# Layer 0 routing and experts in one block, the shared expert under the routing chain

## The reference, cut to what matters

```python
x = layernorm(x + L0_attn(x))
# L0_ffn: 64 experts of width 88, 8 groups of 8 experts, 4 groups and 8 experts kept
scores = sigmoid(x @ gate_w.T);  choice = scores + gate_bias
group_scores = sum of the two largest of choice in each group of 8
masked = choice where the group is among the best 4, else 0
topk_idx = the 8 largest of masked;  topk_w = scores[topk_idx]
rw = topk_w / (sum(topk_w) + 1e-20) * 2.5            # 0 for the other experts
routed = sum_e rw[:, e] * (silu(x @ Wg[e].T) * (x @ Wu[e].T)) @ Wd[e].T
shared = (silu(x @ Sg.T) * (x @ Su.T)) @ Sd.T        # width 176, every token
x = layernorm(x + routed + shared)
```

## Time and profile before

| | |
|---|---|
| median of 3 runs | 1407.01 us (1405.93 to 1410.32) |
| the profiled execution, its own time | 1402.02 us |
| its span | 1400.3 us |
| PE busy over the span | 1279.3 us (91%) |
| DVE | 1114.2 us (80%) |
| ACT | 898.5 us (64%) |
| POOL | 481.3 us (34%) |
| moved by DMA | 135.87 MB |

### The profile page before, as it was taken

How to read it: one execution, slowest core, us unless ns; L and a number is a source line. 1 busy time by engine, 2 the same in 40 slices (tenths; PEclk the granted TensorE clock), 3 DMA queues, 4 the chain that set the end, 5 groups by cost and what they waited for, 6 DMA issues and landing times. The chain is left out here.

```text
span 1400.3 us, 21389 instructions
## 1 busy us (share of the span) xinstructions
PE 1279.3 (91%) x7374; PEld 711.9 (51%) x7374; DVE 1114.2 (80%) x1726; ACT 898.5 (64%) x1503; POOL 481.3 (34%) x988
## 2 busy tenths in 40 slices
PE   5898987169999999999889999999999998999998
PEld 2222224157777777777643232223222337777776
DVE  5677763758999999999758788888889747688886
ACT  4988873034555555555453788888888866767775
POOL 4565551014334343334142244224422422221210
PEclk8898988579999999999999999999999999999999
DMA  5422200064666666666236555434342201121200
GB/s 156 127 56 66 63 21 7 0 134 110 147 143 154 148 151 151 147 146 152 79 113 146 111 156 133 121 102 104 88 123 61 53 11 52 62 91 46 91 31 31
DMA packets 70020, 135.87 MB, mean 97 GB/s; under 512 B 13031, under 2 KB 44328, under 8 KB 63112
## 3 DMA queue, kind: packets, MB, share of 16 engines
q1 hardware_dynamic: 68760, 133.46, 37.5%
q10 hardware_dynamic: 1152, 1.05, 0.2%
HBM read 116.87 MB, written 16.29 MB: 95 GB/s over the span
## 5 line engine op out<-in xcount | busy, mean ns | idle before, releaser
L1589 ACT ACTIVATE a_PR<-n1a_C 128x512 f32<-128x512 f32 x576 | 299.6, 603 | 79.5 <-PE n1a_C L1495 79.4
L1604 DVE CUSTOM_DVE_ANT_0 OC_last<-a_mring,a_COR 128x1024 bf16<-128x1024 f32 x256 | 302.6, 1218 | 42.4 <-PE a_mring L1462 42.1
L1432 POOL TENSOR_SCALAR_AFFINE_SELECT a_PR<-a_PR 128x128 f32<-128x128 f32 x512 | 136.2, 296 | 250.2 <-ACT a_PR L1589 249.7
L868 ACT ACTIVATE e_HH<-e_H 128x512 fp32r<-128x512 f32 x184 | 116.4, 633 | 158.3 <-DVE e_H L916 157.5
L1495 PE MATMUL n1a_C<-a_QP,a_KP 74*128 74x512 bf16 (+3 forms) x768 | 176.1, 332 | 4.4 <-ACT a_PR L1589 3.5
L402 ACT ACTIVATE a_PR<-a_ring,a_ng 128x1024 f32<-128x1024 f32 (+1 forms) x160 | 150.2, 1045 | 26.0 <-PE a_ring L345 26.0
L427 DVE TENSOR_SCALAR a_PR<-a_PR,a_lo,a_hi 128x1024 f32<-128x1024 f32 (+1 forms) x160 | 119.2, 763 | 56.1 <-ACT a_PR L402 55.6
L1514 PE MATMUL n1a_C<-a_PR,a_V 128*9 128x512 f32 (+3 forms) x1536 | 152.1, 492 | 0.0
L887 DVE TENSOR_TENSOR e_HL<-e_H,e_HH 128x512 fp32r<-128x512 f32 x138 | 139.4, 1010 | 13.5 <-DVE e_H L904 0.5
L810 POOL TENSOR_TENSOR e_HL<-e_H,e_HH 128x512 fp32r<-128x512 f32 x46 | 78.5, 1706 | 180.5 <-ACT e_HH L868 180.5
L1883 DVE TENSOR_TENSOR e_HL<-e_GL,e_HH 128x512 fp32r<-128x512 f32 x144 | 109.5, 765 | 38.3 <-ACT e_HH L1851 34.7
(11 more groups left out here) (257 smaller groups left out, 2252.6 us busy)
## 6 DMA issues: line engine op xcount, KB each, us to landing
e_ROUTE<-routing SPq DMA_DIRECT2D x24, 704.0 KB
a_QP<-q_parts SPq DMA_DIRECT2D x72, 192.0 KB
e_RAW<-in_w_chunks SPq DMA_DIRECT2D x46, 192.0 KB, 7.4
a_QM<-q_parts SPq DMA_DIRECT2D x64, 128.0 KB, 2.8
e_GATE<-gates SPq DMA_DIRECT2D x8, 1024.0 KB, 4.4
e_ROUTE<-routing SPq DMA_DIRECT2D x8, 640.0 KB
a_KP<-k_parts SPq DMA_DIRECT2D x24, 192.0 KB
e_ROUTE<-routing SPq DMA_DIRECT2D x8, 576.0 KB
```

Of the source, the lines that this page charges most:

```text
L868: nc.scalar.activation(HH[n % NH][:], HT[n % NH][:], ACT.Copy).then_inc(high_done, 1)
L1432: last = nc.gpsimd.affine_select(out=d, in_=d, compare_op=keep, fill=0.0, base=0, pattern=[[step, P]], channel_multiplier=-step)
L1589: nc.scalar.activation(PR[:, g % NPR, j, :], ring[n % NRING][:], ACT.Exp).then_inc(s_read, 1)
L1604: nc.vector.tensor_tensor_reduce(out=junk[:, i % 2, :], in0=mring[k % 2][:], in1=COR[:, c:c + S], scale=1.0, scalar=-3.0e38, op0=ALU.mult, ...
```

## The change

`route_l0` and `experts_l0` become one block, `moe_l0`, and part of the work in front of it moves into `normalise("n0a")`.

- Inside `n0a`: PE makes the logits of each token group as it is normalised, ACT makes the high half of X and, at the end, the four sigmoids, POOL makes the low half of X and the splits of chunks 0 to 2. SP loads the gate weights and the first four chunks.
- The DVE chain of the routing is rewritten (the two largest of 8 by pairwise maxima and minima), and `link(..., then)` puts products of items into it: 20 in all.
- PE makes gate and up of items 0 to 19 while the chain runs, then turns the routing weights; ACT copies them out of PSUM.
- Items are weighed 20 behind their product (`BEHIND`), their low half follows one item later, `down` runs 23 behind. 24 buffers `T` hold what is between. The shared items are added with one matmul in plain float32 from RAW, without high and low halves.
- There are 4 RAW buffers and 8 slots of split weights, instead of 3 and 3; still 3 buffers `ROUTE`. The low halves on POOL come 6 chunks behind the split. In the last 20 items POOL makes every second low half instead of every fourth.
- In `project_l1` five `keep_busy` matmuls are added behind the third group's `down`, and the last 16 become 5.

```diff
@@ normalise, TensorE, ScalarE, GpSimd
                     spread_inverse(g - 1)
+                    if ahead is not None and g >= 2:
+                        ahead.logits_of(pe, g - 2, done, base + g - 1, C[g - 2])
                 spread_inverse(NG - 1)
+                if ahead is not None:
+                    for g in range(NG - 2, NG):
+                        ahead.logits_of(pe, g, done, base + g + 1, C[g])
...
+                if ahead is not None:
+                    for g in range(NG - 2, NG):
+                        ahead.high_of_x(act, g, done, base + g + 1)
+                    for g in range(NG):
+                        ahead.scores_of(act, g, C[g])
...
+                    for c in range(ahead.FIRST):
+                        ahead.split(pool, c)
+                    for g in range(NG):
+                        ahead.low_of_x(pool, g)
@@ class AheadMoeL0
+    def load_chunk(self, sp, c):
+
+        if c >= NRAW:
+            sp.wait_ge(self.w_split, 2 * (c - NRAW + 1))
+        if NRAW <= c < NRAW + CHS:
+            sp.wait_ge(self.down_done, (c - NRAW + 1) * NG)
+        sp.dma_start(self.RAW[c % NRAW][:], self.a["w_chunks"][c]).then_inc(self.w_loaded[c % NRAW], 16)
+
+    def split(self, pool, c):
+
+        raw, high, low = self.RAW[c % NRAW], self.WH[c % NSLOT], self.WL[c % NSLOT]
+        pool.wait_ge(self.w_loaded[c % NRAW], (c // NRAW + 1) * 16)
+        if c >= NSLOT:
+            pool.wait_ge(self.down_done, (c - NSLOT + 1) * NG)
+        self.nc.gpsimd.tensor_copy(high[:], raw[:]).then_inc(self.w_split, 1)
+        pool.wait_ge(self.w_split, 2 * c + 1)
+        self.nc.gpsimd.tensor_tensor(low[:], raw[:], high[:].bitcast(F32), ALU.subtract).then_inc(self.w_split, 1)
@@ moe_l0 in place of route_l0 and experts_l0
+    NR = 3
+    TURN = 20
+    BEHIND = 20
+    DOWN = BEHIND + 3
+    NTR = 24
+    POOL_BEHIND = 6
+    def on_pool(n):
+
+        return n % NG == 3 or n % NG == 1 and n >= N - BEHIND
...
             @block.sync
             def _(sp):
+                def load_route(c):
+                    if c >= CHS + NR:
+                        sp.wait_ge(h_ready, (c - NR - CHS + 1) * NG)
+                    for e, p0, p1 in segments(c):
+                        sp.dma_start(ROUTE[c % NR][p0:p1], routing[e].partition_broadcast(p1 - p0))\
+                            .then_inc(route_loaded[c % NR], 16)
+
+                for c in range(NRAW, 2 * NRAW):
+                    ahead.load_chunk(sp, c)
                 for g in range(NG):
                     sp.wait_ge(kept, g + 1)
+                    sp.dma_start(routing[:, grp(g)], RT[:, grp(g)]).then_inc(stored, 16)
                 sp.wait_ge(stored, 16 * NG)
+                for c in range(CHS, CHS + NR):
+                    load_route(c)
+                for c in range(2 * NRAW, NCH):
+                    ahead.load_chunk(sp, c)
+                    if c - 2 * NRAW - 1 >= CHS + NR:
+                        load_route(c - 2 * NRAW - 1)
+                for c in range(NCH - 2 * NRAW - 1, NCH):
+                    load_route(c)
 
             @block.gpsimd
             def _(pool):
+                for c in range(ahead.FIRST, NCH + POOL_BEHIND):
+                    if c < NCH:
+                        ahead.split(pool, c)
+                    if c - POOL_BEHIND >= CHS:
+                        for n in range((c - POOL_BEHIND) * NG, (c - POOL_BEHIND + 1) * NG):
+                            if on_pool(n):
+                                low(n)
 
             @block.tensor
...
                 for n in range(N):
+                    if n == TURN:
+                        turn_weights()
...
+                    if 3 <= n < NSH + 3:
+                        down_shared(n - 3)
+                    if n - DOWN >= NSH:
+                        down(n - DOWN)
...
             @block.vector
...
+                for n in range(BEHIND + NSH, N + BEHIND + 1):
+                    if n < N:
+                        product(n)
+                    if n - BEHIND - 1 >= NSH:
+                        low(n - BEHIND - 1)
+                    if n - BEHIND < N:
+                        weigh(n - BEHIND)
@@ project_l1, TensorE
-                        pe.wait_ge(cor_loaded, 32)
...
+                    if g == NG - 2:
+                        pe.wait_ge(cor_loaded, 32)
+                        keep_busy(psV, 5)
...
-                keep_busy(psQ[0], 16)
+                keep_busy(psQ[0], 5)
```

More of the change, by code:

```diff
@@ L727, in experts_l0, with moe_l0 @@
+def moe_l0(nc, X, Y, last_outputs, ahead, consts, routing, part):
+    NR = 3
     NH = 4
-    LAG = 3
+    TURN = 20
+    BEHIND = 20
+    DOWN = BEHIND + 3
+    NTR = 24
     NSH = CHS * NG
@@ new lines, in link @@
+                def link(ins, then=0):
+                    links[0] += 1
+                    ins.then_inc(step, 1)
+                    for _ in range(then):
+                        product(products[0])
+                        products[0] += 1
+                    dve.wait_ge(step, links[0])
+                by_group = ch.rearrange("p t (g e) -> p (t g) e", g=NGRP)
+                flat = lambda t: t[:].rearrange("p t g -> p (t g)")
+                wide = lambda t, k: flat(t).unsqueeze(2).to_broadcast([P, NT_TOK * NGRP, k])
@@ new lines, in _ @@
+                upper = t1.rearrange("p t e -> p (t e)")[:, 0:NT_TOK * NE0 // 2].rearrange("p (g e) -> p g e", e=GSZ // 2)
+                lower = t1.rearrange("p t e -> p (t e)")[:, NT_TOK * NE0 // 2:].rearrange("p (g e) -> p g e", e=GSZ // 2)
+                quarter = lambda n: t2.rearrange("p t e -> p (t e)")[:, n * NT_TOK * NE0 // 4:(n + 1) * NT_TOK * NE0 // 4]\
+                    .rearrange("p (g e) -> p g e", e=GSZ // 4)
+                first, other, third = quarter(0), quarter(1), quarter(2)
@@ new lines, in _ @@
+                dve.wait_ge(ahead.loaded, 48)
+                dve.wait_ge(ahead.scored, NG)
+                link(v.tensor_tensor(ch, sc[:], ahead.bias[:].unsqueeze(1).to_broadcast([P, NT_TOK, NE0]), ALU.add))
+                v.tensor_tensor(upper, by_group[:, :, 0:4], by_group[:, :, 4:8], ALU.max)
+                link(v.tensor_tensor(lower, by_group[:, :, 0:4], by_group[:, :, 4:8], ALU.min), 1)
+                v.tensor_tensor(first, upper[:, :, 0:2], upper[:, :, 2:4], ALU.max)
+                v.tensor_tensor(other, upper[:, :, 0:2], upper[:, :, 2:4], ALU.min)
@@ L1997, in build @@
         with ExitStack() as part:
[L1998 to L2000 removed]
+            ahead0 = AheadMoeL0(nc, part, X, a)
+            normalise(nc, "n0a", X, consts, signals, 0, update=output0, load_ahead=ahead0.load, ahead=ahead0)
+            moe_l0(nc, X, OC, last, ahead0, consts, routing0, part)
             def load_ahead(sp):
```

401 lines of the change are left out of this document (180 added, 221 removed).

## The result

| | us |
|---|---|
| before, median of 4 runs | 1407.80 (1405.93 to 1410.32) |
| after, median of 4 runs | 1446.37 (1442.21 to 1452.28) |
| ratio | 1.0276, 95% interval 1.0233 to 1.0319 |
| predicted | 1414, range 1379 to 1427 |

The change makes the kernel 2.8% slower. The prediction had the direction, but the time lies 32 us above it and outside its range. The profiled execution took 1452.28 (span 1450.3), the slowest of the four.

What follows compares the result with a forecast made beforehand. The prediction took the experts as bound by PE and DVE together, the routing by one engine. 699.8 - 689.3 - 3.5 = +7.0 us on an execution of 1402.02 gave 1409, and 1414 as median; range 1379 to 1427.

Steps and rivals of the forecast that it cites:

- Up to the chain: Normalisation before the routing: with logits and XH moved in, the chain starts at 245.7, 6.9 us earlier.
- The steady part: Chunks 5 to 36: rows asked for too late, DVE waits, 9.2 us a chunk against 8.38; the forecast was staked here.
- The lead is 5.2 us and the same bytes need 7.7: Steady part: rows are asked for 5.2 us before their weighing, but landing takes 7.7, so DVE must wait.
- The ring: Steady part: weighings, POOL's low half and split, SP's issue, landing, next weighing; 18.4 us from one chunk to the chunk after next.
- the 4.9 us of the prediction: Steady part: the skill's formula for 1.245 MB, by which DVE would never wait; the forecast went by the trace's 7.7.
- After chunk 36: From chunk 36's first weighing at 623.4, 20 items at 2.08 us to the last product at 665.
- The end: Last product to Y: ten pairs at 3.2 us and 2.8 more, 34.8 us, bounds 28.8 and 36.
- the exclusion: Last 20 items: POOL's 1.26 us and DVE's two-SBUF-input instructions block each other; a pair at least 3.1, in arrival order 3.3.
- project_l1: Block's end: fewer last keep_busy let ACT end it, -2.0; five added ones may avoid half clock; -3.5 taken, bounds -1.5 and -5.
- Rival A: Steady part: rows arrive in time, a chunk 8.16 to 8.38 us, total 1379 to 1386; chance 0.20.
- The argument against it: Steady part: DMA engines are used 0.66 of the time, 5.5 us of 8.38, so bytes alone exceed the 5.2 us lead.
- Rival B: Under the routing chain: PE gets only the lower clock, 20 items take 51 us instead of 39, +12, 1426; chance 0.08.

Runs made afterwards that it cites:

- rf_bare: rows_first without any product under the routing chain, the 20 products following the chain instead; 1408.72 us, ratio 1.0031.
- late_nopool: The changed kernel with its SP order kept, but POOL makes no low half and DVE makes all; 1419.59 us, ratio 1.0097.
- rows_first: The changed kernel with SP asking for the rows of chunk c-9 ahead of the weights of chunk c; 1388.62 us, ratio 0.9853.
- rf_lag6: rows_first with each chunk's rows asked for six weighings later than their buffer comes free; 1505.71 us, ratio 1.0704.
- rf_swap: rows_first with DVE, for the last 20 items, weighing item k before the low half of item k-1; 1378.83 us, ratio 0.9804.
- rows_half: The changed kernel loading only the first 1024 of 2048 columns of each routing row from chunk 5 on; 1403.54 us, ratio 0.9975.

## Why the prediction was wrong

In "247.4 for 245.7" the measured time comes first and the predicted one second.

**Up to the chain.** Start at 247.4 for 245.7. Ready at 289.7 for 284.9: of the further 3.0 the chain alone cost 1.2 and the products 1.8, as rf_bare shows. Rows asked for at 297.8 for 292, product of item 32 at 325.1 for 317.5: DVE's wait for chunk 8's weights was 9.6, not 5. Together 7.7 us late at chunk 5's first weighing.

**The steady part: the step that failed by its size.** "The lead is 5.2 us and the same bytes need 7.7", so 18.4 us for two chunks. The ring was the right one; late_nopool and rows_first each break one link of it and nearly all waits go. But two chunks took 20.4. Over the 24 chunks whose rows were waited for, the terms are:

| from one first weighing to that of the chunk after the next | predicted | measured, mean |
|---|---|---|
| weighings up to POOL's low half | 7.4 | 7.9 |
| POOL (low half and split) | 3.0, and 0.2 held up | 3.3 |
| SP's reaction | 0.1 | 0.03 |
| landing, from the weights' issue | 7.7 | 9.1 (0.4 and 8.7) |

So the landing is the term that failed: 1.4 of the 1.9 us. I had read it from the wrong row. "2.3/6.9/20.2" in the earlier trace rows is over every load into a tile `e_RAW`, the first ones and those of layer 1 among them. The loads of L778 alone, between 300 and 660 us of the same trace, have

```profile
DMA to landing us min/median/max: 6.0/7.4/8.5
```

and with SP's 0.8 in front that is 8.2, not 7.7. It is also the landing of the weights. By the last semaphore event of each chunk's rows in that trace, the rows land 7.9 us after their first issue (6.6 to 8.8). The other part is the overlap with another chunk's rows: in the changed kernel the 12 late chunks that met none took 8.3 from the rows' issue, the 12 that did 9.0, and rf_lag6, where none meet, has 8.1. This split is a count in one trace and not an experiment. The other terms moved less. DVE holds POOL up in some cycles (3.95 in the one shown, 2.83 where it does not), and the 7.4 is exact behind a long wait and up to 9.1 in other chunks. 31 chunks at 1.0 more are 30 us, most of the miss. DVE's waits for rows, which I had at some 1 us a chunk, were 79.4 in all, 2.4 a chunk.

The Trainium skill ("DMA: Bandwidth & Descriptors", section "Anatomy of one DMA"), whose formula is for another issuing path, leads to the 4.9 us of the prediction; the runs have 9.1 for that transfer, and 5.3 us from the rows' issue at half their bytes.

**After chunk 36.** 36.6 us to the last product for 41.6. I counted 20 items where 19 products stand behind that weighing (2.1 us), and each took 1.93 instead of 2.08. rows_first has 37.8 there.

**The end.** A pair 3.16 for 3.2, the whole 36.6 for 34.8. The value was right and its reason only half: rf_swap shows that the exclusion alone makes 2.88, and the rest is the order on DVE. That the sum of a pair came out was luck in part. The Trainium skill ("SBUF — State Buffer", section "Who interferes with whom") is borne out by that pair: 2.35 for two weighings beside POOL's instruction, 1.28 alone.

**project_l1.** The half clock of the earlier trace rows did go: PE's last values start 45.5 us behind Y instead of 48.1. But I let ACT end the block and did not look at what the attention waits for next. The DMA of q did, and behind PE's idle time there stands the lower clock. Predicted were -3.5; it is about 0 by the other profiles, and +4.8 in the changed kernel's own.

**Sum.** 7.7 + 30.2 - 5.0 + 1.8 = 34.7 at Y, and 8.3 behind it: 43 us in the profiled execution, 1452.3 for 1409. The median lies 6 us below that execution, where I had put it 5 above, so it misses by 32. Rival A's mechanism, rows in time, was right in substance, and its price (1379 to 1386) near what rows_first gives, 1388.6; it just wasn't this kernel. The argument against it held: 0.52 MB are 3.4 us by rows_half, so the bytes alone are some 6.8, over the lead of 5.2. Rival B fell: PE was at the full clock from 270 to 280, under the chain. My upper end of the range came from a chunk of 9.4, a bound that no row supported; with the landing row of 7.4 it would have been near the middle.

## What to carry to other kernels

When a queue's order changes, write down the whole ring (who frees the buffer, who stands in front of the issue, the landing, who waits) and price the landing of the very transfer that will be waited for, from its own line and its own stretch; a median over all loads into a tile of that name mixed in others here. Where nobody waits for it now, the range must leave room for a longer one: 8.2 us became 9.1. Issue the load with the shortest slack first, and never behind a wait that belongs to a load with slack to spare. A long lag between two stages hides stalls, but it is paid back at the end (36.5 us against 5.5 before), where the instruction order of the steady part may be the wrong one.

## What the runs showed that I had not expected

- A low half of 128x512 on POOL costs DVE 1.07 us when DVE has only two-input SBUF work (2.88 against 2.41 a pair), yet without POOL the steady part is slower (9.12 against 8.15 a chunk): there each low half on DVE waits for ACT's rounding, which no row marks as a wait because only 0.1 us of DVE stands idle.
- Behind the waits PE had the lower clock for stretches (0.88 on average from 450 to 500 us), and the ring shows no cost of it: behind a wait the weighings stand 1.99 apart, and POOL's low half comes 7.41 and 7.42 us after the first, with the clock at 0.50 (chunk 19) as at 1.00 (chunk 21).
- The lower clock behind an idle PE is not avoided by filling one gap: with 16 fillers it left 785 to 800 (1.00 for 0.66) and was deeper from 810 to 830 (0.66 for 0.75), and the time was the same.
